# The per-edge weights of a graph layer from 64-row products on the two halves of the array

## What is computed

```python
h_s = s @ lin1_ws * a / 8;  h_v = einsum('nci,cd->ndi', v, lin1_wv) * a / 32**.5   # per node
hid = silu(edge_scalars @ fc_w1 / 8)              # 64 -> 64, per edge
w = hid @ fc_w2 / 8                               # 64 -> 224, per edge
w1, w2, w3, w4, w5 = split(w, [64, 128, 160, 192])
es, ev = h_s[edge_src], h_v[edge_src]             # gather of the source's row
...                                               # messages: w1*es*e0, w2*es x e1, w3*ev*e0, w4*(ev.e1), w5*(ev x e1)
agg = segment_sum(messages, edge_dst)             # per node
...                                               # two linear maps, silu and sigmoid gates
x = layernorm(x + out)
```

## Time and profile before

| | |
|---|---|
| median of 3 runs | 4960.76 us |
| the profiled execution | 4968.59 us, span 4966.8 us |
| PE busy | 4335.4 us (87%) |
| PE weight loads | 1695.4 us (34%) |
| DVE busy | 2456.7 us (49%) |
| ACT busy | 1980.9 us (40%) |
| POOL busy | 2976.9 us (60%) |
| mean granted TensorE clock | 0.970 |
| HBM traffic | 102 GB/s |

### The profile page before, as it was taken

One profiled execution on the slowest core, in us unless ns is written; L12 is line 12 of the kernel. 1 busy time (PEld: TensorE's weight loads), 2 busy tenths in 40 slices (PEclk: granted clock), 3 DMA queues, 4 the chain that ended last, 5 costly groups with the idle time before them and its releaser, 6 DMA issues.

```text
span 4966.8 us, 71591 instructions
## 1 busy us (share of the span) xinstructions
PE 4335.4 (87%) x15455; PEld 1695.4 (34%) x15455; DVE 2456.7 (49%) x7618; ACT 1980.9 (40%) x5183; POOL 2976.9 (60%) x3139
## 2 busy tenths in 40 slices
PE   7888888888888888888888888888888888888887
PEld 6333333333333333333333333333333333333333
DVE  4444555554545454455444545444444444555454
ACT  2343434343434444444434443434343434343434
POOL 1666666666666666666666666666566666666663
PEclk9999999999999999999999999999999999999998
DMA  7333333333333333333333333333333333333333
GB/s 238 94 97 100 98 101 98 103 94 103 98 101 98 101 98 102 96 101 101 97 101 96 102 97 103 98 102 98 99 98 101 98 100 98 100 98 101 99 101 76
DMA packets 395154, 507.25 MB, mean 102 GB/s; under 512 B 71315, under 2 KB 277904, under 8 KB 394724
## 3 DMA queue, kind: packets, MB, share of 16 engines
q0 software_dynamic: 150144, 256.45, 20.4%
q1 hardware_dynamic: 172386, 133.82, 9.3%
q10 hardware_dynamic: 72578, 116.54, 8.1%
HBM read 426.47 MB, written 80.06 MB: 102 GB/s over the span
## 4 chain that ended last, share of the span: by engine, by line
another core or an unknown queue 39%; ACT 23%; issue 16%; PE 15%; SPq 2%; ACTq 1%; DMA 1%; DVE 0%; DVEq 0%
ACT aggsb L681 12%; ACT tsum L686 5%; PE psg L962 5%; PE psg L964 4%; PE pst_e L952 4%; ACT L707 2%; PE psw L943 1%; ACT hid L671 1%; PE psx L933 1%; SPq L549 1%; ACTq L664 1%; DMA agg_table<-aggsb 1%; PE psx L986 1%; SPq L557 0%
## 5 line engine op out<-in xcount | busy, mean ns | idle before, releaser
L637 POOL DMA_INDIRECT rows<-h_table,src_cols x3128 | 2975.4, 951 | 1943.3 <-issue 936.5
L523 DVE TENSOR_TENSOR prod<-psw,rows 128x384 f32<-128x384 f32 (+2 forms) x3128 | 1210.4, 449 | 1616.3 <-remote 863.0
L943 PE MATMUL psw<-fc,hid 128*128 128x480 f32 x3128 | 1473.5, 594 | 2.1 <-ACT hid L671 2.1
L681 ACT ACTIVATE aggsb<-psg 32x160 f32<-32x160 f32 x3128 | 919.2, 294 | 993.3 <-remote 450.8
L962 PE MATMUL psg<-tsum,shifts 128*128 128x448 f32 x1564 | 820.4, 608 | 333.8 <-ACT tsum L686 187.6
L943 PEld LDWEIGHTS psw<-fc,hid 128*128 128x128 f32 x3128 | 532.4, 190 | 926.3 <-issue 908.7
L952 PE MATMUL pst_e<-prod,sel 128*32 128x448 f32 x6256 | 768.2, 564 | 0.0
L964 PE MATMUL psg<-tsum,shifts 128*128 128x448 f32 x1562 | 764.9, 573 | 0.0
L933 PE MATMUL psx<-es,fc 128*128 128x512 f32 x782 | 428.6, 630 | 266.2 <-ACT turned L691 169.9
L686 ACT ACTIVATE tsum<-pst_e 128x448 f32<-128x448 f32 x782 | 425.6, 544 | 349.3 <-remote 210.0
L962 PEld LDWEIGHTS psg<-tsum,shifts 128*128 128x128 f32 x1564 | 246.0, 195 | 771.3 <-ACT tsum L686 364.9
(11 more groups left out here) (112 smaller groups left out, 1468.0 us busy)
## 6 DMA issues: line engine op xcount, KB each, us to landing
es<-in_esP ACTq DMA_DIRECT2D x391, 256.0 KB
agg_table<-aggsb SPq DMA_DIRECT2D x782, 80.0 KB
rows<-h_table,src_cols POOLq DMA_INDIRECT x3128
nag<-agg_table SPq DMA_DIRECT2D x96, 320.0 KB
out<-yn SPq DMA_DIRECT2D x97, 80.0 KB
h_table<-hrow ACTq DMA_DIRECT2D x24, 320.0 KB, 3.1
nxr<-in_x SPq DMA_DIRECT2D x96, 80.0 KB
xa<-in_xT SPq DMA_DIRECT2D x24, 256.0 KB, 2.6
```

The source lines that it names most:

```text
L523: return nc.vector.tensor_tensor(out, w_part, ev, ALU.mult)
L637: nc.gpsimd.indirect_dma_start(out=rows[:, u * QT + j, :], out_offset=None, in_=m.h, in_offset=bass.IndirectOffsetOnAxis(ap=m.src[:, t:t + ...
L681: ins = nc.scalar.activation(aggsb[r, b, :], picked(psg[r, :], k), ACT.Copy)
L943: ins = nc.tensor.matmul(both[:, 0:256 + WN], hid[:, at:at + P], m.fc2[:], start=True, stop=True)
```

## The change

`fc2` shrinks to 128 rows of 224 columns: both halves hold the same matrix, at the same columns. `weights` issues four products for a quad in place of two. Each contracts 64 rows, on the upper half of the array (rows 0 to 63 of `hid` and `fc2`) or the lower, and each streams 224 columns. The upper half writes the quad's first bank of `psw`, the lower half the second, so tile number 2*half+c comes from half `half`, column block c. To match, the host arranges `esP` so that rows 0 to 63 hold tiles 0 and 1 of a quad and rows 64 to 127 tiles 2 and 3, and the alternative branch reads it so. The clearing of `fc2` (L256) goes, since no part of it has to be zero.

```diff
@@ setup_block: loads of the weights
             for src, width in W_ORDER:
-                late.append((m.fc2[r, 256 * half + at:256 * half + at + width], io["fc_w2"][:, src:src + width]))
+                late.append((m.fc2[r, at:at + width], io["fc_w2"][:, src:src + width]))
@@ vector
-            nc.vector.memset(m.fc2[:], 0.0)
             nc.vector.memset(m.fc1[:], 0.0).then_inc(s_fc, 1)
@@ sync, alternative branch
-                    h = S * (u % 2)
-                    sp.dma_start(es[0:S, 0:P], io["esP"][h:h + S, ds(q * CH + P * (u // 2), P)]).then_inc(g_es, 16)
+                    h = S * (u // 2)
+                    sp.dma_start(es[0:S, 0:P], io["esP"][h:h + S, ds(q * CH + P * (u % 2), P)]).then_inc(g_es, 16)
@@ tensor, weights
                 for c in range(2):
-                    both = psw[b][:, 2 * c:2 * c + 2, :].rearrange("p t w -> p (t w)")
                     at = CH * b + P * c
-                    ins = nc.tensor.matmul(both[:, 0:256 + WN], hid[:, at:at + P], m.fc2[:], start=True, stop=True)
+                    for half in range(2):
+                        r = slice(S * half, S * half + S)
+                        ins = nc.tensor.matmul(psw[b][:, 2 * half + c, 0:WN], hid[r, at:at + P], m.fc2[r, :],
+                                               start=True, stop=True)
                 ins.then_inc(w_ready, 1)
@@ build, kernel
-        m.fc2 = sb("fc2", [P, 256 + WN])
+        m.fc2 = sb("fc2", [P, WN])
-        "esP": es.reshape(QUADS, 2, 2, P, S).transpose(2, 4, 0, 1, 3).reshape(2 * S, QUADS * CH),
+        "esP": es.reshape(QUADS, 2, 2, P, S).transpose(1, 4, 0, 2, 3).reshape(2 * S, QUADS * CH),
```

## The result

The changed kernel takes 5221.62 us (median of 4 runs, 5185.51 to 5240.18) against 4964.57 us (4960.44 to 4976.75) of the kernel before: ratio 1.0505, 95% interval 1.0444 to 1.0565. The forecast was 4967 us, with a range from 4938 to 5003, so it was wrong.

The account below looks back on a forecast made before the run. GpSimd's list was taken to bound the kernel. The profiled 4968.6 us, less 13 of relief in long waits, plus 19 for a lower clock, gave 4975; for the median, 4960.8 + 6 = 4967 us, range 4938 to 5003.

Parts of the forecast that it names:

- the first part: What bounds the kernel: GpSimd's list from end to end; a faster TensorE can win at most 27 us of waits.
- the fourth part: TensorE idles 2.0 to 2.2 us before `psg`, its clock may fall: 0.40 us a step, 19 us taken, 0 to 39.
- the batch of rows 4: Profiled batch: TensorE idle 1.35 us between `psw` and `psg`, GpSimd pausing 2.67 us; one such step in each 8-quad round.
- Second part: `psw` on TensorE: 0.75 us of paired passes plus 0.22 for the shape change, against 1.61; gain 0.64 us a quad.
- Rival (c): The array's halves work in turn: 0.11 us more a quad, no more idle time; 4964 us, chance 0.07.
- Third part: Shorter `psw` relieves GpSimd's 22 waits over 2.8 us: 13 us won, bounds 0 and 27.
- the step with `node_lin`: TensorE runs without pause from `psw` to the tile sums; GpSimd's 3.10 us wait there should lose its 0.58 us excess.
- Rival (a): The clock decides: more idle time lowers TensorE's clock; slower, 4991 us up to 5055, chance 0.30.
- point of decision: The clock was to decide once it falls in about 57 of the 97 steps, at 0.40 us each.
- Rival (b): Relief of GpSimd's long waits alone, clock falling no more often: 13 to 27 us faster, about 4940 us, chance 0.15.
- Rival (d): TensorE, 87% busy, is the bound: 500 us less, 4461 us, chance 0.03.

Follow-up runs that it names:

- e6: Kernel before with one gather a quad in place of four once the ring is full; 4060.28 us, ratio 0.9919.
- e7: Changed kernel with one gather a quad in place of four once the ring is full; 3556.28 us, ratio 0.8689 to the kernel before.
- e2: Kernel before with products of 288 in place of 480 columns, still four passes a quad; ratio 0.9981.
- e15: Kernel before with one of a quad's two weight products left out after the first ones; 4883.55 us, ratio 0.9951.
- e9: Changed kernel unaltered, on a chip where the kernel before takes 4096.74 us; 4123.12 us, ratio 1.0067.
- e1: Kernel before with four products of all 128 rows and 224 columns a quad, in place of two of 480; ratio 1.0394.
- e3: Changed kernel with one more product of 128 rows and 256 columns a quad, its result overwritten; ratio 1.0992 to the kernel before.
- e4: Kernel before with two more products of 8 columns a quad, into PSUM columns that nothing reads; ratio 1.0736.
- e13: Kernel before with GpSimd waiting for VectorE's products in place of TensorE's tile sums; 5863.89 us, ratio 1.1948.
- e12: e3 again, on a chip where the kernel before takes 4096.74 us; 4096.16 us, ratio 1.0000.

## Why the prediction was wrong

Two steps failed, one behind the other. The first is a reading in the first part: "So there is a floor of about 2.52 us after a batch, whatever TensorE does". The sum around it was right and closed again, and the number held (2.55 us after the change, without the long waits). But it is no property of GpSimd: it is the time until TensorE's signal comes, some 2.3 us after the batch, though the work was done 1.7 us before GpSimd moved. I asked no further who else waits for such signals. ScalarE's 2.20 us before the copy are the same thing.

The second is the term that this left wrong, the price in the fourth part: one step in a round, 0.40 us, 39 us at most. It held the lateness of the copy fixed ("the copy comes no earlier") and put at nothing, without a reason, that it could come later. The runs showed that it does, by 4.57 us in the batch above and by over 3 us in 91 places in place of 6; TensorE's next sums are late with it, and GpSimd's wait is over 2.8 us in 133 places in place of 22. A round has four waits. In the one that I had priced, that of the batch of rows 4, 67 of 97 became long, against the 48 that I took, but with 123 us of excess, 1.8 us each in place of 0.40. The one after it, for which I had no term, has 48 long waits and 155 us. None of my rivals had this.

Second part: right. The passes run in pairs, and 0.75 and 0.22 us are confirmed in their sum by e6 and e7, to 0.005 us a quad. Rival (c) is out.

Third part, relief of 13 us: not seen. The wait behind the step with `node_lin` was long 14 times before, with 13 us of excess, and is so after the change. In e2, which shortens `psw` as much, 3 of the 14 are left, so the reasoning was fair where nothing else changes; but 24 waits of the batch after it are long there, and the excess of e2 is 16 us in all.

Fourth part, apart from its price: the right sign, and a chain that exists, but as a link behind another cause. The clock fell further than forecast (0.901), in 227 stretches against 76, and the chain that I described (idle before `psg`, a lower clock, late sums) is in 119 of the 133 long waits. But I let the idle time grow by what `psw` loses, 0.7 us. A `psw` as short as that does no harm in e2 (155 stretches) or e15 (205, and faster than before). What opens the gap is the late copy, 4 us of idle time where I had 2.0 to 2.2. Rival (a), "the clock decides", to which I gave 0.30 and up to 5055 us, had the last link and about a third of the size (5055 - 4961 = 94 of 257 us); its point of decision, counted in steps of the short `psw`, is refuted by e2.

Rival (b), faster by the relief, is out. Rival (d) is out on the first kind by the sum. On the second kind too: TensorE freed of 500 us, and e9 no faster.

Shown: the loss is GpSimd's waits; it needs a chip of the first kind; it comes with TensorE's instructions (e1, e3, e4; the passes and their weight loads were only changed together) and not with a shorter `psw` and its idle time (e2); the copies that come late are there in each kernel that loses and nearly absent in those that don't. Inferred from the semaphore records, and borne out by e13: TensorE's signals land late while gathers run. Read from the trace and not tested by a run of its own: that the clock, fallen behind the wait for the copy, makes up to 174 us of the loss. Open: what holds the signals, why more passes make them later inside a batch, and whether the recording of a profile has a part in it; every run of this study was recorded alike, so that can't be told here. The traces of the first kind lack records of semaphores, and not of TensorE's alone: the kernel before has 456 of 782 for `prod_ready` of VectorE and 402 for `tsum_copied` of ScalarE, e13 596 for `w_ready`; those of the second kind are nearly complete (770 of `w_ready` in e9). The counts of late signals rest on the records that are there; those of late copies do not. Open too: whether the kind belongs to the chip or to the time of the measurement, since none of these chips was measured at two times.

## What to carry to other kernels

A pause that the view puts down to an engine that had long been done is not a property of the engine that waits: ask what delays the signal, and which other waits hang on signals of the same engine, even where the pause itself stays as it is. Splitting a matmul into more instructions can lose even where it saves 40% of its time, so the number of instructions on TensorE belongs in the sum where its signals are late; a kernel with the count changed and the work kept tests it. And measure on more than one chip, with the kernel before beside it: the same edit gave 1.050 and 1.007, another 1.195 and 0.999.

## What was not expected of the hardware

- Chips differ: the kernel before takes 4907 to 4981 us on some and 4093 to 4097 us on others, 16 to 18% less, with nearly the same gathers (0.95 us each). The difference is the 389 pauses, 2.59 us against 0.32 in e12: 389 x 2.27 = 883 us, less 13 us of longer gathers, where the medians differ by 868 us (4964.57 and 4096.74).
- On the first kind `w_ready` is 5.5 us late at the 95th percentile before and 6.8 us after the change, while VectorE's and ScalarE's signals are 0.01 us behind. A batch of eight gathers takes 9.7 to 9.9 us, and nearly all late signals of `w_ready` come some 2.2 us after its end, not in it.
- A signal was held longer without more work on TensorE: the copy is over 3 us late 64 times with 8 passes of 224 columns over all rows (1.50 us a quad, e1) and 6 times with 4 of 480 (1.61 us).
- A clock of 0.917 on average, at its lower level for some 810 of 4881 us, did not make e15 slower, where a late copy stood before it 5 times; behind a late copy the step took 4.20 us in place of 2.66.
- A gather takes 964 ns on average beside the changed kernel's TensorE and 955 ns with one more product there (e9, e12).
